# Local attention layers on one Trainium2 core: the scores of a tile in two halves, with a later tile's query projection between them

## What is computed

```python
DEPTH, HEADS, DIM_HEAD, WINDOW = 6, 16, 64, 32
def attn_layer(x, Wqkv, qs, ksc, Wo):
    q, k, v = heads of x @ Wqkv
    q = rotary(l2norm(q) * qs);  k = rotary(l2norm(k) * ksc)
    # each window of 32 queries sees its own 32 keys and the 32 before them
    sim = einsum('bhwie,bhwje->bhwij', bq, bk2) * 8.0     # masked
    attn = softmax(sim)
    return (attn @ bv2) @ Wo
def ffn_layer(x, ...):
    a, gate = split(layernorm(x) @ W1 + b1)
    return a * gelu(gate) @ W2 + b2
for i in range(DEPTH):
    x = attn_layer(shift_tokens(x), ...) + x
    x = ffn_layer(shift_tokens(x), ...) + x
```

## Time and profile before

| what | value |
|---|---|
| median of three runs | 2007.75 us (2005.34 to 2017.78) |
| profiled execution | 2002.5 us |
| its span, first to last instruction | 2000.6 us |
| mean granted TensorE clock | 0.982 |
| PE busy | 1837.5 us (92%) |
| DVE, POOL, ACT busy | 1539.0, 1468.6, 1293.8 us (77%, 73%, 65%) |
| chain that ended last | PE 59%, POOL 8%, issue 6%, DVE 2%, ACT 2% of the span |
| scores L584, matmuls | 12288, 149.8 us busy, 40.7 us idle before them, 30.6 of it "issue" |

### The profile page before, as it was taken

One profiled execution on the slowest core, in us unless ns is written; L12 is line 12 of the kernel. 1 busy time (PEld: TensorE's weight loads), 2 busy tenths in 40 slices (PEclk: granted clock), 3 DMA queues, 4 the chain that ended last, 5 costly groups with the idle time before them and its releaser, 6 DMA issues.

```text
span 2000.6 us, 61664 instructions
## 1 busy us (share of the span) xinstructions
PE 1837.5 (92%) x24771; PEld 1251.1 (63%) x24771; DVE 1539.0 (77%) x2364; ACT 1293.8 (65%) x1858; POOL 1468.6 (73%) x2112
## 2 busy tenths in 40 slices
PE   5789999996799999999999999999999999999987
PEld 2455555554566666666666676666666667776665
DVE  2345454446989988998898998999889989898962
ACT  3567777753556766766776677666667766766652
POOL 3344444447898888898887888888888889888850
PEclk8899999998899999999999999999999999999999
DMA  3999999972000200011000110002000020000000
GB/s 125 280 356 358 339 355 341 360 253 64 5 15 16 65 13 12 12 50 33 12 14 12 54 27 12 14 13 67 14 12 13 12 69 13 12 14 13 12 13 24
DMA packets 111850, 175.06 MB, mean 88 GB/s; under 512 B 51748, under 2 KB 75216, under 8 KB 110800
## 3 DMA queue, kind: packets, MB, share of 16 engines
q1 hardware_dynamic: 111568, 171.12, 27.4%
HBM read 87.06 MB, written 68.29 MB: 78 GB/s over the span
## 4 chain that ended last, share of the span: by engine, by line
PE 59%; POOL 8%; issue 6%; DVE 2%; ACT 2%; POOLq 0%; DVEq 0%; ACTq 0%
PE tpose L614 14%; PE ring L540 14%; PE ring L598 8%; PE ring L550 6%; PE ring L633 6%; PE ring L584 6%; PE yps L643 3%; POOL roped L250 2%; POOL roped L332 2%; POOL probs L338 1%; DVE turned L708 1%; ACT qT L400 1%; PE ring L570 1%; DVE ss L723 1%; PE yps L624 1%
## 5 line engine op out<-in xcount | busy, mean ns | idle before, releaser
L708 DVE TENSOR_TENSOR turned<-ring,ropes 128x1024 f32<-128x1024 f32 x384 | 450.5, 1215 | 45.5 <-PE ring L540 45.4
L250 POOL TENSOR_TENSOR roped<-turned 128x512 f32<-128x512 f32 x288 | 384.9, 1358 | 29.7 <-DVE turned L708 29.7
L614 PEld LDWEIGHTS tpose<-wvo,oT 128*128 128x128 f32 x3072 | 366.9, 193 | 43.0 <-issue 35.1
L614 PE MATMUL tpose<-wvo,oT 128*128 128x128 f32 x3072 | 378.4, 277 | 4.9 <-ACT oT L434 4.7
L540 PE MATMUL ring<-wqk,xT 128*128 128x512 f32 x768 | 377.5, 615 | 5.5 <-ACT xT L394 3.8
L332 POOL TENSOR_TENSOR roped<-roped,rnorm 128x1024 f32<-128x1024 f32 x192 | 361.7, 1905 | 7.6
L1236 POOL TENSOR_SCALAR less<-less,lowest 128x512 f32<-128x512 f32 x256 | 174.4, 692 | 239.8 <-DVE lowest L1205 239.8
L1205 DVE CUSTOM_DVE_ANT_0 less<-ps_b,shifted 128x512 f32<-128x512 f32 x256 | 166.6, 688 | 221.4 <-PE ps_b L1068 80.3
L383 ACT ACTIVATE squares<-ring 128x1024 f32<-128x1024 f32 x192 | 197.6, 1029 | 95.2 <-DVE turned L708 95.2
L723 DVE TENSOR_REDUCE ss<-squares 128x16 f32<-128x1024 f32 x192 | 232.3, 1210 | 32.8 <-ACT squares L383 32.8
L434 ACT COPY oT<-ring 128x1024 f32<-128x1024 f32 x192 | 185.0, 1015 | 78.9 <-PE ring L598 78.7
(11 more groups left out here) (136 smaller groups left out, 2978.4 us busy)
## 6 DMA issues: line engine op xcount, KB each, us to landing
shifted<-scratch_w SPq DMA_DIRECT2D x64, 1024.0 KB, 11.8
scratch_w<-wrows SPq DMA_DIRECT2D x48, 1026.0 KB, 10.0
scratch_w<-x SPq DMA_DIRECT2D x16, 1026.0 KB, 9.8
wqk<-in_l_wqkv SPq DMA_DIRECT2D x6, 1024.0 KB, 5.4
xs<-xs SPq DMA_DIRECT2D x96, 48.0 KB, 1.9
wv<-in_l_wqkv SPq DMA_DIRECT2D x6, 512.0 KB
wo<-in_l_wo SPq DMA_DIRECT2D x24, 128.0 KB
xs<-x SPq DMA_DIRECT2D x96, 32.0 KB
```

Source lines behind the costliest of these rows:

```text
L250: engine.tensor_tensor(halves[2][:, :, side, :], halves[0][:, :, side, :], halves[1][:, :, 1 - side, :], ALU.add).then_inc(done, 1)
L614: last = nc.tensor.matmul(out[:, 0:D], oT[:, h, :], wvo[:, layer_of(t), r, j, :], start=h == 0, stop=h == HEADS - 1)
L708: ins = nc.vector.tensor_tensor(turned[:, n, part, :].rearrange("p (h d) -> p h d", d=DH), heads, table, ALU.mult)
```

## The change

`scores(n)` becomes `scores(n, 0)` and `scores(n, 1)`, four head pairs (32 matmuls) each. The waits and the taking of the room stay with the first half, the count of `scored` goes to the end of the second. `project("Q", n + 2)`, which stood behind all of the scores, now stands between the halves. Nothing is computed more or less, and no other engine's list changes.

```diff
-            def scores(t):
-                if live(t):
-                    pe.wait_ge(s["qT_copied"], t + 1)
-                    pe.wait_ge(s["kT_copied"], t + 1)
-                    pe.wait_ge(s["masked"], t + 1)
-                    out = take("S", t)
-                    for j in range(PAIRS):
+            def scores(t, half):
+                if live(t):
+                    if half == 0:
+                        pe.wait_ge(s["qT_copied"], t + 1)
+                        pe.wait_ge(s["kT_copied"], t + 1)
+                        pe.wait_ge(s["masked"], t + 1)
+                        take("S", t)
+                    out = view("S")
+                    for j in range(half * PAIRS // 2, (half + 1) * PAIRS // 2):
...
-                    last.then_inc(s["scored"], 1)
+                    if half == 1:
+                        last.then_inc(s["scored"], 1)
...
                 attend(n - 3)
-                scores(n)
+                scores(n, 0)
                 project("Q", n + 2)
+                scores(n, 1)
                 if step == 1:
                     project_ffn(g - 3)
```

## The result

The changed kernel takes 2142.69 us (median of four runs, 2138.42 to 2149.32) against 2007.55 us before (2005.34 to 2017.78): ratio 1.0667 with a 95% interval of [1.0629, 1.0705], 134 us slower by the ratio, 135 by the medians. The forecast was 2142 us, range 2085 to 2190. The profiled execution took 2141.51 us, its span 2139.7 us at a mean granted clock of 0.983, practically that of before (0.982). So the sum came out. Two of its terms did not, in opposite directions: the steps behave as forecast, but that the total is met this closely is luck.

A forecast was written before the change was run, and what follows sets the result against it. PE (TensorE) was taken to bound every step. Step costs of 161.7 us, plus 3 for the first twelve tiles, less 31 of fetch gaps, gave +134 on 2007.75, thus 2142 us; range for 8 in 10: 2085 to 2190.

The forecast's parts named there:

- Q and the copy of OB: After the first half of the scores, Q still waits for ACT's copy of OB, starting 1.41 us in; PE idles about 0.7 us per tile.
- The changes of form: Two more switches between whole-array and part-array matmuls around the second half of the scores, 0.10 us each per tile.
- What is queued behind: Scores end 2.62 us later, delaying DVE and ACT work: steps 0 and 2 +2.38, step 3 +2.26, step 1 +0.90 us.
- The fetches: PE's gaps inside the scores and before a projection, taken for late instruction fetches: all 31.3 us regained, 0 as other bound.
- The early tiles: First twelve tiles, without feed-forward and waiting for POOL: 14.56 us each against a new floor of 14.78, 12 x 0.2 = 3.
- the clock stayed at 1.00: Against the rival that gaps in every period drop PE's clock, 0.94 over the layers: 2183 us; chance 0.05.
- the gaps did not stay: Against the rival that half a tile's scores still exhaust a late-requested instruction block: +165, 2173 us; chance 0.12.
- PE's list alone: Rival: the waits for square and gate have more slack, all steps pay only 0.90 us: +46, 2054 us; chance 0.08.
- a faster kernel: Rival: fetch gaps of 31.3 us go and the later end of the scores costs nothing: 1976 us; chance 0.07.

## Why the prediction held, point by point

*Q and the copy of OB.* "1.41, between 1.14 and 1.41" was 1.29: the copy ends 1.15 us after the scores' start, and Q starts 0.14 us behind it. The idle time of 0.4 to 0.6 us before L540 on 91 tiles is as foretold.

*The changes of form.* 0.10 us each was about right: Q takes 1.89 us up to the second half (1.82 + 0.07), the half 0.79 (0.70 + 0.09), and at step 1 the feed-forward behind it 2.78 instead of 2.68. The maximum came 2.58 us later (1.52 to 4.10), forecast 2.62.

*What is queued behind.* Undisturbed steps 0 and 2 pay 2.33 us each, step 3 2.22, step 1 0.84 (shortest periods before and after), forecast 2.38, 2.26 and 0.90. The runs with the split at some steps alone confirm these as causes, not only as sizes. On step 3 the prediction was right about the size and short on the reason (timeline of the changed kernel, the step 3 that starts at 1198.70):

```profile
1205.30 1.06 ACT L416 ACTIVATE probs<-probs 128x1024 f32<-128x1024 f32 x1 [4.53 <-DVE probs L740]
...
1206.37 1.28 ACT L475 ACT_TABLE_LOAD   x1
...
1207.67 0.69 ACT L475 ACTIVATE gelu<-ring,b 114x512 f32<-114x512 f32 x1
...
1208.57 0.74 DVE L797 SCALAR_TENSOR_TENSOR hT<-ring,b,gelu 114x512 f32<-114x512 f32 x1
...
1209.46 1.06 PE L550 MATMUL ring<-ident,roped 128*128 128x128 f32 x8 [1.20 <-DVE hT L797]
```

Gelu, queued behind the exponentials and a load of its table of 1.28 us, ends at 1208.36, 0.21 us ahead of the gate. Moving the gate forward on DVE alone could therefore gain 0.2 us at most; that was not tried.

*The fetches.* All of the 30.5 us went, as assumed, and by the trace they were late fetches. Somewhat more went with them: the steps' growth alone is 20 x (2.33 + 0.84 + 2.33 + 2.22) = 154.4 us between tiles 12 and 92, and that stretch grew by 119.8, so 34.6 us came back, where 31 was the forecast. Part of the difference is the clock, which the prediction had at 1.00: behind the gaps of tiles 37 and 76 before, it was at its lower level for a while (0.72 in the 6.2 us from Q on in tile 37), and Q took 2.76 and 3.38 us instead of 1.82. After, it stayed at 1.00 from tile 12 to tile 92. POOL's few waits there went too.

*The early tiles* are the failed step: "12 x 0.2 = 3" was 18.1 us in the trace and 21 us in the run with these tiles alone. The mean of eight periods mixed in a step 3, and the first four tiles were not looked at, though no work there covers a delay of `scored`: a quarter of those twelve tiles pays 2.5 us or more each.

So +119.8 stands where 130 was forecast for those 80 periods (158.4 less 28 of gaps), the rest of the layers grew by 2.0, and the early tiles by 18.1: +139 us of span against a forecast of +134, the low term and the high ones nearly cancelling by luck. Of the rivals, the clock stayed at 1.00, the gaps did not stay, PE's list alone would have been 2054 us, and for a faster kernel Q would have had to start at 0.70 us and not at 1.29.

## What to carry over

Work that is moved between a producer's pieces delays the consumer by its whole length and by what it waits for there (here 2.58 us for a Q of 1.82); what it costs is that delay less the slack of each step, so read the slack step by step in the shortest periods, and also at the start, where pipelines run without cover. Before filling a gap, find out what makes it: here 30 us of idle time that a filler removes at 160 us of delay could be had, two thirds of it, by shifting where instruction blocks end. A change that adds instructions anywhere ahead of such a stretch moves those places; here that alone gained or lost one per cent.

## What the runs showed of the hardware

- A stretch of 256 TensorE instructions in 1.41 us can outrun the instruction fetch when a block of 256 ends late in it: TensorE goes on 1.14 to 1.60 us after the 16 KB packet has landed, and a late block cost 0.3 to 2.8 us. The Trainium skill, Runtime: NRT & Kernel Launch, Instruction fetch mechanics, gives the block as 16 KiB of 256 instructions and its crossing as mostly hidden; the size agrees with the gaps at 193 or 194 modulo 256, the hiding does not: by place alone the time went from 0.990 to 1.0105 of the kernel before.
- Empty instructions put in by an alignment directive are not free on TensorE: some 314 in a group of four tiles (512 less 412, 462, 421 and 439), 7,624 in the trace. They follow each other in 0.07 us (101 in 7.5 us in tile 36), and the run took 448 us more (2461.48 - 2012.95), part of it at a lower granted clock, 0.91 instead of 0.98.
- A matmul that waits for three semaphores started 0.14 us after the end of the ACT copy it waited for; changes between whole-array and part-array matmuls cost 0.07 us ahead of the second half, 0.09 behind it and 0.10 at the feed-forward, and with the feed-forward between the halves the two more changes cost 0.37 us together.
